# Self-attention softmax sums as columns: small reciprocal, gathered into rows by DMA, spread by a product, with new orders

## What is computed

```python
def _attn(xq, ctx, wq, wkv, wo, bo):
    q = _heads(xq @ wq)                       # 16 heads of 64
    k, v = jnp.split(ctx @ wkv, 2, axis=-1)
    q = _rope(q, sq, cq); k = _rope(k, sk, ck)
    sim = jnp.einsum('bhnd,bhmd->bhnm', q, k) * DH ** (-0.5)
    a = jax.nn.softmax(sim, axis=-1)
    o = jnp.einsum('bhnm,bhmd->bhnd', a, v)
    return o.reshape(...) @ wo + bo

x = _attn(attn_in, attn_in, sa_wq, sa_wkv, sa_wo, sa_bo) + x      # self: the stage changed
x = _attn(cross_in, ctx_n, ca_wq, ca_wkv, ca_wo, ca_bo) + x
x = gelu(ffn_in @ ff_w1 + ff_b1) @ ff_w2 + ff_b2 + x
```

## Time and profile before

| what | value |
|---|---|
| median of 3 runs | 1935.18 us (1932.8 to 1937.34) |
| the profiled execution, first to last instruction | 1934.6 us |
| TensorE busy | 1889.5 us, 98% |
| VectorE busy | 1582.3 us, 82% |
| ScalarE busy | 945.2 us, 49% |
| GpSimd busy | 1266.3 us, 65% |

### The profile page before, as it was taken

The page is one execution under the profiler, slowest core; times in us unless marked ns, Lnnn a source line. Parts: engine busy times, 40 slices in busy tenths (PEclk is TensorE's granted clock), DMA queues, the critical chain, the costliest instruction groups (busy, mean ns, idle before and its releaser), DMA issues.

```text
span 1934.6 us, 52084 instructions
## 1 busy us (share of the span) xinstructions
PE 1889.5 (98%) x19952; PEld 1289.2 (67%) x19952; DVE 1582.3 (82%) x2316; ACT 945.2 (49%) x1460; POOL 1266.3 (65%) x816
## 2 busy tenths in 40 slices
PE   7999999979999999999999999999999999999999
PEld 5666767745666666666666666666666666666664
DVE  4999999967888888888888888888888888888842
ACT  3555545533545444445554445455444445544444
POOL 4777756415776676677767677776776667667661
PEclk8999999978999999999999999999999999999999
DMA  5332233211111111111111111111111111111100
GB/s 176 117 88 86 81 112 88 73 33 48 53 54 53 55 51 53 59 55 54 54 51 55 52 58 57 51 56 51 55 50 56 57 54 56 51 53 52 53 29 23
DMA packets 147729, 119.07 MB, mean 62 GB/s; under 512 B 63392, under 2 KB 111648, under 8 KB 147488
## 3 DMA queue, kind: packets, MB, share of 16 engines
q1 hardware_dynamic: 110624, 115.46, 17.9%
q10 hardware_dynamic: 36864, 0.28, 1.0%
HBM read 36.71 MB, written 1.05 MB: 20 GB/s over the span
## 4 chain that ended last, share of the span: by engine, by line
PE 87%; POOL 4%; issue 3%; DVE 3%; DMA 1%; ACT 1%; SPq 0%; ACTq 0%; DVEq 0%; POOLq 0%
PE S L1376 24%; PE OB L1390 20%; PE PB L1338 10%; PE PB L1325 10%; PE S L1357 7%; PE PB L1399 2%; PE PB L1310 2%; PE S L1225 2%; PE PB L1409 1%; PE PB L1191 1%; PE OB L1253 1%; PE OB L1236 1%; DMA swapped<-turned 1%; POOL KL L667 1%; POOL psum_acc L674 1%
## 5 line engine op out<-in xcount | busy, mean ns | idle before, releaser
L708 POOL TENSOR_TENSOR psum_acc<-psum_acc,P 124x1024 f32<-124x1024 f32 (+1 forms) x320 | 689.8, 2156 | 216.9 <-ACT P L851 207.4
L851 ACT ACTIVATE P<-S 124x1024 f32<-124x1024 f32 (+1 forms) x448 | 431.3, 963 | 514.6 <-PE S L1376 513.9
L1069 DVE TENSOR_REDUCE mxc<-S 128x2 f32<-128x1024 f32 x384 | 470.0, 1224 | 94.9 <-PE S L1357 88.1
L1390 PE MATMUL OB<-P,V 124*64 124x256 f32 (+1 forms) x3328 | 437.3, 387 | 0.0
L1390 PEld LDWEIGHTS OB<-P,V 124*64 124x64 f32 (+1 forms) x3328 | 221.4, 137 | 188.7 <-issue 104.8
L701 POOL TENSOR_TENSOR psum_acc<-P 124x1024 f32<-124x1024 f32 x64 | 152.0, 2374 | 213.4 <-ACT P L851 213.4
L1376 PE MATMUL S<-QH,KH 64*124 64x256 f32 (+1 forms) x1664 | 271.8, 323 | 5.8 <-ACT P L851 5.8
L728 ACT ACTIVATE V<-PB 124x512 f32<-124x512 f32 (+1 forms) x320 | 157.2, 491 | 206.4 <-PE PB L1338 167.0
L1376 PEld LDWEIGHTS S<-QH,KH 64*124 64x124 f32 (+1 forms) x1664 | 154.0, 181 | 128.5 <-issue 104.7
L1376 PE MATMUL S<-QL,KH 64*124 64x256 f32 (+1 forms) x1664 | 235.2, 278 | 0.0
L1376 PE MATMUL S<-MX,share 64*124 64x256 f32 (+1 forms) x1664 | 235.0, 278 | 0.0
(11 more groups left out here) (159 smaller groups left out, 2844.8 us busy)
## 6 DMA issues: line engine op xcount, KB each, us to landing
swapped<-turned SPq DMA_DIRECT2D x512, 128.0 KB, 2.1
kv_w<-sa_kv_dram SPq DMA_DIRECT2D x64, 128.0 KB, 2.3
qswapped<-qturned SPq DMA_DIRECT2D x128, 64.0 KB, 1.9
kv_w<-ca_kv_dram SPq DMA_DIRECT2D x64, 96.0 KB, 2.2
ctxT_all<-ctx_dram SPq DMA_DIRECT2D x8, 624.0 KB, 4.4
q_w<-sa_wq_dram SPq DMA_DIRECT2D x64, 64.0 KB, 2.0
q_w<-ca_wq_dram SPq DMA_DIRECT2D x64, 64.0 KB, 2.0
o_w<-ca_wo_dram SPq DMA_DIRECT2D x64, 64.0 KB, 2.0
```

The costliest lines, as they stand in the source:

```text
L708: pool.tensor_tensor(acc, acc, P_of(J, c)[0:rows, :, 0:w], ALU.add).then_inc(x.acc, 1)
L851: act.activation(P_of(J, c)[0:rows, :, 0:w], SP[0:rows, :, 0:w], ACT.Exp, scale=SCALE).then_inc(x.e, 1)
L1069: dve.tensor_reduce(mxc[:, t, :, c:c + 1], MP[:, :, 0:w], AX.X, ALU.max).then_inc(x.am, 1)
L1390: ins = pe.matmul(OB[half(h), 0:N], Vb[J % 2][0:w, t, half(h)], P_of(J, c)[0:w, h, k * N:(k + 1) * N], start=(t == 0), stop=(t == len(a_.t ...
```

## The change

For the first 60 of the 64 steps (J < DIRECT) the sums are made and inverted in another shape:

- `sums` now uses the folded P as the stationary operand and one column of ones as the moving one: eight products, each of 64 queries, give XB[:, 0:4], a 128x4 tile with one sum in each place.
- `invert` takes the reciprocal of these 128x4 into a small SBUF tile.
- a new word `i` on SP issues two DMAs that gather it into row 0 of two 128x256 tiles, zero elsewhere.
- a new word `bc` on TensorE multiplies ones (128x64) by these tiles: XB again holds the inverse on all partitions, for `divide`.

The orders of all five engines are written anew. In the last four steps the sums are made as before, and `divide` follows `invert` at once (except in the last). The zeroed tiles are the buffers of the cross stage's rotated queries, set at the start.

```diff
-                 "qk+3 ln+3 o+-2 p+-1 sum+-1 v+2 s a+2 ct n",
-                 "c+2 ln+2 am+1 ad+-2 r+2 t+3 rc+-1 dv+-1 cn n",
-                 "mr+1 ve+2 e ca cn ln+3 h+3 oe",
-                 "f cp l+3 cc+3 cq",
-                 "w+4 x+3")
+                 "ln+3 qk+3 bc+-2 p+-1 sum+-1 v+2 o+-2 s a+2 n ct",
+                 "am+1 r+2 dv+-2 t+3 rc+-1 c+3 ln+6 cn ad+-2 n",
+                 "h+2 ve+2 ln+3 e cn ca mr+2 oe",
+                 "cp f+1 cq cc+3 l+3",
+                 "x+2 w+5 i+-1")
...
+        MIs = [q[:, :] for q in qrotb]
+        inverses_s = nmxc[1][:, :, :].bitcast(F32)
...
+        DIRECT = STEPS - 4
...
+            def self_inverse_rows(J, _):
+
+                if J < DIRECT:
+                    wait(sp, z.inv, J + 1)
+                    wait(sp, s_bc, J)
+                    if J == 0:
+                        sp.wait_ge(s_rows, 7)
+                    for h in range(2):
+                        sp.dma_start(MIs[h][0:1, :], inverses_s[:, h, :]).then_inc(s_ir, 16)
...
+            for h in range(2):
+                pool.memset(MIs[h], 0.0).then_inc(s_rows, 1)
...
                 def invert(J, _):
                     wait(dve, z.sum, J + 1)
-                    dve.reciprocal(XB[:, 0:N], XB[:, 0:N]).then_inc(z.inv, 1)
+                    if J < DIRECT:
+                        wait(dve, s_ir, J * 32)
+                        dve.reciprocal(inverses_s.rearrange("p h t -> p (h t)"), XB[:, 0:4]).then_inc(z.inv, 1)
+                    else:
+                        dve.reciprocal(XB[:, 0:N], XB[:, 0:N]).then_inc(z.inv, 1)
+                    if DIRECT <= J < STEPS - 1:
+                        divide(J, 0)
 
                 def divide(J, _):
                     wait(dve, z.inv, J + 1)
+                    if J < DIRECT:
+                        wait(dve, s_bc, J + 1)
...
+                def divide_spread(J, _):
+                    if J < DIRECT or J == STEPS - 1:
+                        divide(J, 0)
...
-                readers = {"sum": (z.ot, lambda K, k: K + 1),
+                readers = {"sum": (None, lambda K, k: (z.inv if K < DIRECT else z.ot, K + 1)),
+                           "bc": (z.ot, lambda K, k: K + 1 if K < DIRECT else None),
                            "o": (z.added, lambda K, k: K // 2 + 1 if K % 2 else None)}
...
                 def sums(J, _):
                     wait(pe, z.f, J + 1)
                     x_free(uses, readers, J, ("sum", 0))
-                    for h in range(2):
-                        ins = pe.matmul(XB[half(h), 0:N], onesw[:, :], added_up(J)[:, h, :], start=True, stop=True)
+                    if J < DIRECT:
+                        for h in range(2):
+                            for t in range(2):
+                                for a in range(2):
+                                    ins = pe.matmul(XB[half(a), 2 * h + t:2 * h + t + 1],
+                                                    added_up(J)[:, h, t + a * D:(a + 1) * D:2], onesw[:, 0:1],
+                                                    start=True, stop=True)
+                    else:
+                        for h in range(2):
+                            ins = pe.matmul(XB[half(h), 0:N], onesw[:, :], added_up(J)[:, h, :], start=True, stop=True)
                     ins.then_inc(z.sum, 1)
+
+                def spread_inverse(J, _):
+                    if J < DIRECT:
+                        wait(pe, s_ir, J * 32 + 32)
+                        x_free(uses, readers, J, ("bc", 0))
+                        for h in range(2):
+                            ins = pe.matmul(XB[half(h), 0:N], onesw[:, :], MIs[h], start=True, stop=True)
+                        ins.then_inc(s_bc, 1)
```

More of the change, by code:

```diff
@@ L25, with __init__ @@
 class Stage:
-    def __init__(self, name, pe, dve, act, pool, sp, xuses=("sum", "o")):
+    def __init__(self, name, pe, dve, act, pool, sp, xuses=("sum", "bc", "o")):
         self.name = name
@@ L175, in block_kernel @@
         s_set = sem("constants_set")
+        s_ir = sem("self_inverse_rows")
+        s_bc = sem("self_inverse_spread")
         s_rows = sem("stack_rows_set")
@@ L509, in self_swap @@
                     sp.dma_start(rope[:, lo:hi], rope_in[:, lo:hi]).then_inc(s_rope, 16)
-            run_steps(SELF, in_order(SELF.sp, {"w": self_weights, "x": self_swap}))
+            def self_inverse_rows(J, _):
[6 more added lines that the diff above has]
+                        sp.dma_start(MIs[h][0:1, :], inverses_s[:, h, :]).then_inc(s_ir, 16)
+            run_steps(SELF, in_order(SELF.sp, {"w": self_weights, "x": self_swap, "i": self_inverse_rows}))
             def cross_weights(J, pair):
@@ L1006, in self_attention @@
                 words = {"ln": in_first(FIRST_DVE, {**norm(LN1), "ada": adaln_vectors}), "n": in_ramp(RAMP_DVE, do), "cn": context_inverse, "t": turn, "c": cosines, "r": rotate, "am": maximum,
-                                                    "rc": invert, "dv": divide, "ad": add}
+                                                    "rc": invert, "dv": divide_spread, "ad": add}
                 run_steps(SELF, in_order(SELF.dve, words), False)
@@ L1169, in x_free @@
                     value = value(K, k)
+                    if isinstance(value, tuple):
+                        semaphore, value = value
                     if value is not None:
@@ L1284, in self_attention @@
                 words = {"ln": in_first(FIRST_PE, {**ln1, "mean": mean}), "qk": project, "v": project_v, "a": max_scores, "s": scores, "p": products,
-                         "sum": sums, "o": output, "ct": transposes, "n": in_ramp(RAMP_PE, do)}
+                         "sum": sums, "bc": spread_inverse, "o": output, "ct": transposes, "n": in_ramp(RAMP_PE, do)}
                 run_steps(SELF, in_order(SELF.pe, words), False)
```

## The result

The changed kernel takes 2005.42 us (median of four runs, 2003.04 to 2008.48) against 1936.26 for the kernel before beside it: 1.0364 times, 95% interval 1.0351 to 1.0378. Forecast were 1969, range 1934 to 1994: the direction and the mechanism were right, the size was half, and the time lies outside the range.

The account below looks back on a forecast made before the run. The prediction took VectorE, then TensorE, to pace the self-attention stage; afterwards a 5.83 us ring in plain steps and 6.2 in turn steps give +30, slow transfers +4: 1934.6 + 34, rounded to 1969 us, range 1934 to 1994.

Parts of the forecast that it names:

- What bounds the kernel: Self-attention stage: VectorE sets the pace first, TensorE later; the small reciprocal frees 97 us of VectorE, with TensorE close behind.
- The ring (where i stands): SyncE's queue: the next swap waits behind the gathers, closing a one-step loop through VectorE and TensorE; 5.83 us, 5.45 to 6.45.
- Sum over the steps: Self-attention stage: 29 plain steps at 5.83, 30 turn steps at 6.2, plus 2, giving 357.1 us against 327.0: +30.
- Slow issues and landings: Transfers in the steps: slow ones lose their cover in plain steps and partly in the others; +4 us, bounds 0 to +15.
- Other orders: Remaining order changes on the engines, with the last four steps keeping the full reciprocal: together 0, bounds -3 and +3 us.
- The range: Whole kernel: 1934 to 1994 us; the likeliest case alone 1949 to 1990, its lower end from 5.55 plain and 6.15 turn.
- Sixteen rows in 0.45 us: Sums on TensorE: eight one-column products make sixteen rows in 0.45 us, with a tail 0.62 to the signal.
- D: Rival for the sums on TensorE: one-column products issued singly, 1.0 us, ring 6.28, +57 us, 1992; chance 0.08.
- B: Rival: TensorE alone paces since the gathers' issues cost SyncE little; 5.14 a plain step, +9 us, 1944; chance 0.11.
- C: Rival: faster, as TensorE's waits for VectorE vanish with the long reciprocal; -11 us, 1924; chance 0.13.
- Spread product 0.43 in turn steps: TensorE: the new product spreading the inverses is pure addition, 0.43 us, bounds 0.43 and 0.62; turn steps carry it.

Follow-up runs that it names:

- e4: Changed kernel without the gathers: the spread product multiplies a zero tile, so the output is not scaled by the sums; 1962.0 us, ratio 1.0134.
- e17: Changed kernel with only VectorE's order altered: division ahead of the rotate, small reciprocal ahead of the turn; 1969.8 us, ratio 1.0172.
- e19: e17 with one gather of 512 values a step instead of two; 1967.6 us, ratio 1.0166.
- e3: Changed kernel with two more gathers a step, read by nobody, behind the two real ones on SyncE's queue; 2082.7 us, ratio 1.0754.
- e16: e15 with the spread product cut from 256 columns to one, output not scaled; 1956.3 us, ratio 1.0122.
- e15: e4 with the sums made by the two wide products instead of sixteen one-column rows; 1963.9 us, ratio 1.0156.
- e10: Changed kernel with the two gathers of a step issued by ScalarE instead of SyncE; 1996.2 us, ratio 1.0310.
- e1: Changed kernel with SyncE issuing the swap of step j+3 ahead of the gathers of step j-1; 1995.2 us, ratio 1.0309.

## Why the prediction was right or wrong

- *What bounds the kernel:* right. Once the gathers are harmless (e4, e17 to e19) TensorE paces (busy 340.1 of 351.0 us in e19's stage) and VectorE's 84 us are worth nothing.
- *The ring (where i stands):* right, link by link. Terms, forecast and then measured in the step shown above: rotate to sums 1.12, 1.16; sums to the first gather's issue 0.87, 0.90; issues of i 1.11, 1.19; first issue of x 0.53, 0.64; landing 2.15, 2.10; signal 0.05, 0.08. Sum 5.83, measured 6.07; the shortest step is 6.02. The swap issued behind a gather takes 0.60 to 0.65 where it took 0.53.
- *Sum over the steps:* 357.1 without the allowance for slow transfers. At the shortest step 59 x 6.03 = 355.8. The ring was 0.2 longer than I had it in plain steps, and TensorE seldom the bound in turn steps, where I gave it 6.2: it waits for the division in 46 of the 59. The two errors cancel.
- *Slow issues and landings, +4, bounds 0 to 15:* this is the step that failed. They cost 387.2 - 355.8 = 31.4 us; the 29 steps whose issues (second gather, swap) and landing are together within 0.3 us of their least carry only 2.8 of it. I argued that cover is lost in part; in a ring that paces every step there is no cover, and each extra microsecond is paid in full. The slow cases themselves were there before: the kernel before has 28 landings of the swap over 2.6 us in its 59 steps, the changed one 25. The median of an issue was the wrong figure, since the ring pays the mean: issues and landings together 0.45 us a step above their medians.
- *Other orders, 0 within 3:* failed too, by a smaller sum: +6.8 behind the steps. I left the last four steps aside since they keep the full reciprocal, and did not ask what is queued behind it in the new order: the output product. The +2.1 ahead of the steps can't be told from nothing: that stretch, 46.8 us here, is 44.4 to 49.5 in the experiments.
- *The range:* its lower end of 1949 is a wrong sum. 29 x 5.55 + 30 x 6.15 + 2 is 347.5, so +20 and 1955. The measured time lies far on the other side.
- *Sixteen rows in 0.45 us:* right, 124.47 to 124.94 is 0.47. D, which needed 1.0, did not come. The Trainium skill's floor of some 62 ns a MATMUL with hardware decode off (TensorE: Matmul & The Clock Gate, Back-to-back issue gap) is not seen in these rows, which come at 29 ns each on alternating column halves.
- *B:* the right account of the kernel without gathers, but 18 us too low (1944 against 1962): 5.35 a plain step instead of 5.14, and 9 us around the steps. The sentence from the Trainium skill that would have spoken for it (DMA: Bandwidth & Descriptors, Issuing engines are not separate DMA queues), that a sequencer's time to start a DMA is usually small relative to the DMA, does not hold here: e3 has 1.25 us a step for two issues against a landing of 2.1.
- *C:* did not come; it needed the ring under 5.5 and a TensorE with waits to lose, and even e16 stays above the kernel before.
- *Spread product 0.43 in turn steps:* right as a duration, here read in a plain step (128.81 to 129.24); 7.7 us in effect (e15, e16).

## What to carry to other kernels

Before a transfer is put into a queue, write down the order on every engine that it connects and look for a way round that comes back after one step. If there is one, add its links by their means and not their medians, because nothing hides the tail. Then try the cheapest cut first: here two exchanges in VectorE's order gave back more (36 us) than halving the gathers did (26), and two cuts that each helped made a new ring together. A short operation in place of a long one gains only as far as the next engine is behind, and here that was TensorE, nearly at once.

## What the runs showed of the hardware

- An issue on SyncE's queue takes 0.47 to 0.60 us in the median of a run's swaps or gathers. Back to back, some 0.65 from start to start, they add up one for one: +1.25 us for two (e3).
- All 490 issues of over 0.9 us, in 18 profiles, began within 1.3 us of an instruction packet's start (22 to 36% of all issues did), and 480 of 481 late landings of the swap had one beside them. The number of packets does not order the runs: 27 packets on q8 went with 28 and with 12 late landings, 35 with 25 and with 10.
- Small gathers issued on ScalarE's queue while SyncE issues the swap and weights land after 2.5 us instead of 2.0 (e10); behind transfers of 400 KB on their own queue after 3.6 (e1).
